# Scores issued one pair further ahead in the attention loops of a small language tower

## The reference, cut to what matters

```
# four layers, 12 heads of 16, window 64, per batch of 256 tokens
scores = q @ k.T / sqrt(16);  scores = where(|i - j| <= 64, scores, -1e9)
probs  = softmax(scores);     out = probs @ v
# the last attention: the same with 12 heads and no window, once
```

## Time and profile before

| what | value |
|---|---|
| three runs | 1853.67, 1856.35, 1860.24 us; median 1856.35 us |
| the profiled execution | 1862.7 us, its span 1860.9 us |
| mean granted TensorE clock | 0.889 |
| attention passes, first to last scores (us from the span's start) | 80.5 to 221.6, 331.2 to 471.0, 580.6 to 721.5, 827.2 to 965.4, 1386.3 to 1527.9 |

### The profile page before, as it was taken

How to read it: one execution, slowest core, us unless ns; L and a number is a source line. 1 busy time by engine, 2 the same in 40 slices (tenths; PEclk the granted TensorE clock), 3 DMA queues, 4 the chain that set the end, 5 groups by cost and what they waited for, 6 DMA issues and landing times.

```text
span 1860.9 us, 42615 instructions
## 1 busy us (share of the span) xinstructions
PE 1476.6 (79%) x13098; PEld 1249.1 (67%) x13098; DVE 1252.3 (67%) x3542; ACT 978.7 (53%) x2392; POOL 811.5 (44%) x1177
## 2 busy tenths in 40 slices
PE   0588889789898988998888759759758987589991
PEld 0367678677676776777777748539737766489991
DVE  4698966789676989669896652434378997434444
ACT  0478733688434886348873223226438982156550
POOL 5576333685235763247733310125446521145540
PEclk9899989899898998999998957669959996689996
DMA  4665201734005560025520000047535411267765
GB/s 111 174 149 116 47 1 33 172 87 85 1 5 133 103 134 2 1 66 145 119 44 1 1 14 0 21 155 216 167 93 119 103 37 35 81 198 242 234 211 178
DMA packets 144317, 178.26 MB, mean 96 GB/s; under 512 B 22096, under 2 KB 106128, under 8 KB 143952
## 3 DMA queue, kind: packets, MB, share of 16 engines
q1 hardware_dynamic: 136784, 158.18, 33.0%
q0 software_dynamic: 7296, 17.18, 2.8%
HBM read 132.96 MB, written 42.34 MB: 94 GB/s over the span
## 4 chain that ended last, share of the span: by engine, by line
PE 29%; DVE 12%; issue 5%; POOL 3%; DMA 3%; ACT 2%; SPq 0%; POOLq 0%; DVEq 0%; ACTq 0%
PE bank L1472 7%; DVE neg_max L791 2%; PE bank L1458 2%; PE bank L645 1%; PE bank L1459 1%; PE bank L1461 1%; PE bank L1460 1%; PE bank L1462 1%; DVE xn L911 1%; PE bank L1216 1%; PE bank L431 1%; DVE ptl L798 1%; PE bank L1445 1%; DMA kx<-qk_rows 1%; DMA xn<-y_rows 1%
## 5 line engine op out<-in xcount | busy, mean ns | idle before, releaser
L685 ACT ACTIVATE prob<-bank,neg_max 128x192 f32<-128x192 f32 (+1 forms) x960 | 361.9, 433 | 77.3 <-DVE neg_max L791 65.6
L791 DVE TENSOR_REDUCE neg_max<-bank 128x2 f32<-128x384 f32 (+1 forms) x480 | 275.6, 575 | 46.1 <-PE bank L544 39.2
L798 DVE TENSOR_TENSOR ptl<-bank,pth 128x384 f16<-128x384 f32 (+1 forms) x480 | 274.9, 573 | 39.6 <-ACT pth L698 26.0
L563 PE MATMUL bank<-ident,prob 128*128 128x128 f32 x1536 | 269.3, 289 | 0.0
L698 ACT ACTIVATE pth<-bank 128x384 f16<-128x384 f32 (+1 forms) x480 | 249.4, 520 | 34.2 <-PE bank L563 29.0
L652 ACT ACTIVATE xx<-bank 128x256 fp32r<-128x256 f32 x256 | 94.5, 383 | 196.8 <-PE bank L431 193.0
L544 PE MATMUL bank<-kx,qx 96*128 96x192 bf16 (+1 forms) x960 | 168.1, 257 | 1.1 <-DVE xx L765 1.1
L563 PEld LDWEIGHTS bank<-ident,prob 128*128 128x128 f32 x1536 | 163.4, 143 | 0.1
L584 PE MATMUL bank<-v,pth 128*128 128x33 bf16 x1152 | 138.7, 180 | 17.0 <-DVE ptl L798 12.0
L542 PE MATMUL bank<-mask,ident 128*128 128x384 bf16 x384 | 130.7, 340 | 20.8 <-DMA kx<-qk_rows 11.7
L733 ACT ACTIVATE fbuf<-bank,b 128x512 f32<-128x512 f32 x96 | 65.8, 687 | 146.4 <-PE bank L453 146.4
(11 more groups left out here) (295 smaller groups left out, 4537.2 us busy)
## 6 DMA issues: line engine op xcount, KB each, us to landing
xn<-in_e_seg SPq DMA_DIRECT2D x34, 768.0 KB, 6.6
w<-in_e_w SPq DMA_DIRECT2D x23, 576.0 KB, 4.2
qk_rows<-fbuf SPq DMA_DIRECT2D x128, 96.0 KB, 2.3
qx<-qk_rows SPq DMA_DIRECT2D x35, 288.0 KB, 4.1
kx<-qk_rows SPq DMA_DIRECT2D x35, 288.0 KB, 5.8
qk_rows<-w SPq DMA_DIRECT2D x80, 96.0 KB, 2.3
qx<-qk_rows SPq DMA_DIRECT2D x35, 192.0 KB, 4.7
kx<-qk_rows SPq DMA_DIRECT2D x35, 192.0 KB, 5.5
```

The source lines that it names most:

```text
L563: last = nc.tensor.transpose(bank[BT[p % 2]][:, c * P:c * P + P], probs_at(p, banded, c * P, P), ident[:, :])
L685: nc.scalar.activation(probs_at(p, banded, qt * n, n), scores_at(p, n)[:, qt, :], ACT.Exp, bias=neg_max[:, b % 2, hd, qt:qt + 1], scale=1. ...
L791: nc.vector.tensor_reduce(neg_max[:, b % 2, hd, :], scores_at(p, D if banded else S), AX.X, ALU.max, negate=True).then_inc(max_ready.sem, 1)
L798: nc.vector.tensor_tensor(ptl[:, p % 2, 0:n], bank[BT[p % 2]][:, 0:n], pth[:, p % 3, 0:n], ALU.subtract)\
```

## The change

The scores move one iteration ahead of where they were. Iteration 0 now issues the scores of pairs 0 and 1, iteration p those of pair p+1. Products, transposes and steps stay where they were, and no other engine's list changes; all waits inside pe_scores stay as they are, so the scores issued in iteration p wait for the exponentials of pair p-2, and the first scores of a batch wait for its DMAs one iteration earlier.

```
             for p in range(PAIRS + 5):
-                if p < PAIRS:
-                    pe_scores(pe, it, p, banded)
+                for ahead in ((0, 1) if p == 0 else (p + 1,)):
+                    if ahead < PAIRS:
+                        pe_scores(pe, it, ahead, banded)
                 if p >= 5:
                     pe_values(pe, it, p - 5, banded)
                 if p == 3:
                     pe.wait_ge(y_read.sem, y_read.at(it, 0))
                 if 0 <= p - 3 < PAIRS:
                     pe_turn_probs(pe, it, p - 3, banded)
                 pe_step(pe, it, p, banded, w, w_out, tile, xx)
```

## The result

| | before | changed |
|---|---|---|
| median of 4 runs each, same chip | 1856.42 us (1853.67 to 1860.24) | 1868.40 us (1866.47 to 1871.18) |
| the profiled execution, its span | 1862.7, 1860.9 us | 1869.7, 1867.9 us |
| mean granted TensorE clock | 0.889 | 0.891 |

The changed kernel takes 1.0066 of the time of before, interval 1.0042 to 1.0090: 12 us longer, where 1871 us were forecast.

The account below looks back on a forecast made before the run. No engine is full; a ring of short hand-offs between three nearly full engines bounds each pass. Terms 8 + 2 + 3 + 2 + 1 - 1 = 15 us, put on the median 1856.35, give 1871 us; range 1853 to 1890.

Parts of the forecast that it names:

- GpSimd's chain: GpSimd's copies of middle values wait for later products and lead to batch 4's DMAs: 1 us lost, bounds 0 and 1.6.
- No gain from earlier maxima: VectorE's 39.2 us of waits for scores shrink, but it changes one idle for another: 1 us gained, bounds 0 and 9.
- The new wait in the banded passes: Scores(p+1) wait for exp(p-2) ahead of products and transposes, delaying hi: 22 us, a third kept, 8 us; bounds 0 and 22.
- mixtures: Banded passes: new path of 1.18 us a pair binds only with a v step on TensorE or VectorE's six-head sums behind it.
- the covered rival: Late hi is absorbed by VectorE's extra work, and the DMA is late by itself: 0 to 5 us, 1858; chance 0.24.
- Fifth pass: New ring through exp, scores and transposes takes 1.35 us a pair against 1.34; with VectorE's sums 2 us lost, bounds 0 and 4.5.
- DMA wait at scores(48): Banded passes: TensorE's wait for batch 4's DMAs moves ahead of products(42) and transposes(44): 3 us lost over four passes.
- Scores(72): Banded passes: the DMA wait at these scores comes an iteration earlier: 2 us lost for four passes, bounds 0 and 4.
- SyncE's reads: Reads of odd batches wait for earlier scores and can go an iteration sooner; these batches don't wait for DMAs: nothing.
- Clock: Gaps at batch 4's DMAs grow some 0.6 us; if TensorE came back at half rate in all four passes, 2 us more.
- What the waits showed: Sign: TensorE's score waits for exponentials rise to tens of us, VectorE's for scores fall, its hi or ScalarE's transpose waits rise.
- passes that get shorter: Sign against the prediction, which had passes growing by about 15 us: each banded one 2 to 5, the fifth 1 to 4.

## Why the prediction was right

The mechanism forecast, the new wait ahead of products and transposes, is the one found, and the total is near: 15 us forecast, measured 12 (interval 8 to 17). That the total is so near is partly luck. The terms that the runs bear out were 8 + 2 - 1 = 9 us; the 6 us of DMA waits and GpSimd's chain, which made it 15, were not found. Step by step:

- **No gain from earlier maxima (1 us taken).** Right. The scores behind the transposes give them at no price, and the time stays (0.9998). VectorE exchanged one idle for another, as the earlier trace rows had let one expect.
- **The new wait in the banded passes (8 us, bounds 0 and 22).** Right in kind and size: +0.43% (0.25 to 0.62), 8 us, where only later halves have it; 7.0 to 7.8 us in the profiles. The place was right too: what stays is lost where VectorE's sums of six heads hold up the exponentials and a step stands behind on TensorE, the "mixtures" of the prediction. Two things were off. It said that behind chunks exp(p-2) is over when TensorE comes; that holds for the next iteration, but scores(54) wait 0.27 us for exp(51), which costs nothing in the end. And it counted four whole passes, while the first halves cost nothing measurable: TensorE stands at the DMAs of batch 4 there anyhow, so the covered rival was right for that half. The third of 22 us that was kept was a choice and not worked out; that 8 was forecast for whole passes and 8 measured for half of them is luck.
- **Fifth pass (2 us, bounds 0 and 4.5).** Within its bounds by time: 0.15% (0 to 0.30), 3 us, in the experiment on it alone. The profiles have +5.6, +1.9, and +3.3 us with this pass alone. Not foreseen was the idle time between the products of scores(49), up to 1.45 us.
- **DMA wait at scores(48) (3 us).** Not confirmed. In the profiles that stretch did not grow; the experiment that leaves these scores in place points to a price by its time and to none by its profile.
- **Scores(72) (2 us).** Nothing. Transposes(57) to (81) hold them and take 31.5, 31.5, 31.5 and 31.4 us before, the fourth with its DMA wait of 0.57 us no longer than the others: what is lost there is made up by (81). With these scores in their old place and all else ahead, the stretch was as long as in the changed kernel.
- **GpSimd's chain (1 us).** Not found: scores(48), which wait for the DMAs of batch 4, start no later behind the first scores of a pass, but for 0.4 us in one of eight cases, and in the third pass 3.4 and 3.8 us sooner. Whether SyncE's reads, which can go an iteration sooner and which the prediction put at nothing, have a part in that is not shown.
- **Clock (2 us more, outside the sum).** Wrong, and so was the reading under it. I took the level from the first product behind a gap, 0.34 us in the second pass, as full. TensorE before, the same pass, the next chunk and mask product:
```profile
409.00 0.63 PE L453 MATMUL bank<-xx,wa_second_lo 128*128 128x512 f32 x1
409.43 0.54 PE L542 MATMUL bank<-mask,ident 128*128 128x384 bf16 x1
```
At full clock these take 0.40 and 0.34. In this profile the clock had fallen in all four passes, behind the gap or within 1.5 us of work; the row to read is the granted clock of the stretch. And the gaps did not get longer in sum, 7.6 and 10.8 us in the two profiles, against 11.1 and 11.2 before: the prediction moved TensorE's last work one iteration earlier, but left out that the new wait makes TensorE arrive later. Whether the low level comes varies between executions of one kernel (four passes and two before, one and two after), so how much of its cost lies in either kernel's median is not known.

What the waits showed is what the prediction had asked for; the growth of the passes was 15 forecast, and 6.3 and 8.8 in the two pairs of profiles (590.1 + 154.0 against 589.4 + 148.4, and 592.8 + 150.3 against 585.9 + 148.4), while the medians moved by 12. The prediction had named passes that get shorter as a sign against it, and three of eight did, by 0.6, 2.6 and 0.6 us; there the time up to transposes(47), with the landing of batch 4 in it, shrank by more than the later half grew. The settled terms, 7 to 8 us in the later halves and 2 to 3 in the fifth pass, make 9 to 11 of the 12. The rest is inside the intervals and stays open.

## What to carry to other kernels

Work moved ahead in the list of an in-order engine takes its waits with it, past everything that stands behind. Ask what the others wait for in that list (here the transposes), and put the early work behind it: there the same move was free. A delay in front of a transfer whose landing hangs on another engine need not cost anything. An idle gap in front of dense matrix work can cost more than its length; filling this one paid 0.33%.

## What the runs showed of the hardware

- A wait added to TensorE's list made the kernel faster (0.9977 in all passes, 0.9959 in the first halves of the banded passes only). A shorter idle gap ahead of scores(48) and the clock behind it were the reason expected; the profiles do not prove it.
- Behind gaps of 3.19 and 2.25 us the first mask product took 0.50 us; behind 2.56 and 3.09 it took 0.34 and 0.32, and the clock fell 1.2 and 1.5 us later. In the second profile of the same kernel it fell behind 3.02 and 2.79 us and not behind 2.59 and 2.82. Behind the changed kernel's gaps of 1.68, 2.05 and 1.38 us it did not fall in that stretch, behind 2.48 it did (0.48 us); again, it fell behind 3.95 and 3.02 and not behind 2.40 and 1.44. So the length of the gap alone does not tell. Twelve products without use in the gap, 2.11 us in one row, kept it up in all four passes; their row, and the scores behind, in the first pass:
```profile
152.41 2.11 PE L605 MATMUL bank<-mask,ident 128*128 128x384 bf16 x12
155.40 0.34 PE L542 MATMUL bank<-mask,ident 128*128 128x384 bf16 x1 [0.88 <-DMA kx<-qk_rows]
```
